# TensorE's side products cut into single matmuls and laid out anew in every step; ScalarE copies the value bank out ahead of that block's first exponential

## The reference

```python
xn = group_norm(x)                                   # 32 groups, no gain
xs = reshape(xn, (B, T, C))                          # B 16, T 1024, C 512
q, k, v = (einsum('btc,hcd->bhtd', xs, W) for W in (Wq, Wk, Wv))   # 8 heads of 64
att = softmax(einsum('bhtd,bhsd->bhts', q, k) / 8, axis=-1)
out = einsum('bhts,bhsd->bhtd', att, v)              # 1024 x 1024 scores per head
out = transpose(out, (0, 2, 1, 3)).reshape(B, T, -1) @ Wproj + bproj
return x + reshape(out, (B, C, H, W))
```

## Time and profile before

| | us |
|---|---|
| median of 3 runs (4952.30 to 4955.85) | 4953.66 |
| the profiled execution, first to last instruction | 4946.9 |
| PE busy | 4705.1 (95%) |
| ACT busy | 2886.6 (58%) |
| DVE busy | 2775.5 (56%) |
| POOL busy | 2326.6 (47%) |

### The profile page before, as it was taken

The page is one execution under the profiler, slowest core; times in us unless marked ns, Lnnn a source line. Parts: engine busy times, 40 slices in busy tenths (PEclk is TensorE's granted clock), DMA queues, the critical chain, the costliest instruction groups (busy, mean ns, idle before and its releaser), DMA issues.

```text
span 4946.9 us, 73065 instructions
## 1 busy us (share of the span) xinstructions
PE 4705.1 (95%) x20608; PEld 3505.4 (71%) x20608; DVE 2775.5 (56%) x5284; ACT 2886.6 (58%) x5507; POOL 2326.6 (47%) x1837
## 2 busy tenths in 40 slices
PE   7999999999999999999999999999999999999998
PEld 5777767777676776767767677676776767767675
DVE  5655646556465564655646556465564655646454
ACT  4665646556465564655646566464664646656465
POOL 2444545445454454544545445454444545445455
PEclk9999999999999999999999999999999999999999
DMA  2111111111111111111111111211112111111101
GB/s 69 34 37 55 31 53 35 46 46 32 52 34 50 43 34 54 31 53 41 32 54 35 51 41 30 63 28 53 37 30 62 35 49 35 32 61 34 53 23 51
DMA packets 156934, 212.71 MB, mean 43 GB/s; under 512 B 56544, under 2 KB 57568, under 8 KB 156512
## 3 DMA queue, kind: packets, MB, share of 16 engines
...
## 4 chain that ended last, share of the span: by engine, by line
issue 50%; POOL 42%; PE 6%; POOLq 1%; ACT 1%; DVE 0%; DMA 0%; SPq 0%; ACTq 0%; DVEq 0%
POOL prob_l L1031 32%; POOL o L1048 6%; POOL res L1054 3%; PE bank L517 1%; PE bank L561 1%; POOLq L1030 1%; POOL rstd L1023 1%; PE bank L578 1%; PE bank L690 1%; PE bank L692 1%; PE bank L691 1%; PE bank L571 0%; PE bank L572 0%; POOLq L1047 0%; DMA xs<-in_x 0%
## 5 line engine op out<-in xcount | busy, mean ns | idle before, releaser
L1031 POOL TENSOR_TENSOR prob_l<-prob,prob_h 128x512 fp32r<-128x512 f32 x1408 | 1803.5, 1288 | 2470.5 <-ACT prob_h L710 2452.6
L710 ACT ACTIVATE prob<-bank 128x512 f32<-128x512 f32 x2048 | 1237.6, 604 | 1698.6 <-PE bank L572 1579.3
L864 DVE TENSOR_REDUCE smax<-bank 128x1 f32<-128x512 f32 x2048 | 1349.1, 684 | 1012.6 <-PE bank L578 997.8
L710 ACT ACTIVATE prob_h<-bank 128x512 fp32r<-128x512 f32 x2048 | 1236.7, 604 | 198.6 <-PE bank L692 154.9
L690 PE MATMUL bank<-prob_h,vh 128*128 128x512 f32 x2048 | 832.6, 407 | 117.9 <-ACT acc L781 99.3
L578 PE MATMUL bank<-k_hl,q_hh 128*128 128x512 f32 x2048 | 802.5, 436 | 33.6 <-DVE smax L864 30.4
L571 PE MATMUL bank<-q_hh,k_hl 128*128 128x512 f32 x2048 | 824.0, 402 | 0.5 <-ACT prob_h L710 0.5
L572 PE MATMUL bank<-q_lm,k_h 65*128 65x512 f32 x2048 | 813.8, 397 | 0.0
L692 PE MATMUL bank<-prob_l,vh 128*128 128x512 f32 x2048 | 809.6, 395 | 0.0
L691 PE MATMUL bank<-prob_h,vl 128*128 128x512 f32 x2048 | 809.0, 395 | 0.0
L803 DVE TENSOR_TENSOR prob_l<-prob,prob_h 128x512 fp32r<-128x512 f32 x640 | 508.0, 804 | 511.9 <-ACT prob_h L710 511.8
...
## 6 DMA issues: line engine op xcount, KB each, us to landing
xs<-in_x SPq DMA_DIRECT2D x128, 256.0 KB, 2.8
q_hh<-q_hh SPq DMA_DIRECT2D x256, 128.0 KB, 2.2
k_hl<-k_h SPq DMA_DIRECT2D x256, 128.0 KB, 2.4
inv_b<-inv_dram SPq DMA_DIRECT2D x256, 128.0 KB, 2.8
res<-in_x SPq DMA_DIRECT2D x128, 256.0 KB, 2.7
out_x<-res SPq DMA_DIRECT2D x128, 256.0 KB, 2.0
q_lm<-q_lm SPq DMA_DIRECT2D x256, 2.0 KB
den<-acc SPq DMA_DIRECT2D x256, 2.0 KB, 1.7
```

Source lines behind the costliest of these rows:

```text
L710: return nc.scalar.activation(out, ps[ST + bank][:, :], ACT.Exp, scale=SCALE)
L864: nc.vector.tensor_reduce(smax[:, j:j + 1], ps[SM + j % 2][:, :], AX.X, ALU.max).then_inc(rows_used, 1)
L1031: nc.gpsimd.tensor_tensor(prob_l[:, r3, :], prob[:, ring2, :], prob_h[:, r3, :].bitcast(F32), ALU.subtract).then_inc(prob_l_pool, 1)
```

## The change

- `WORK` gives, for each slot, a tuple of pieces (kind, half, number of single matmuls, bank); row products are pieces too (`("row", n)`) and `MAXIMA` is gone. A projection can stop after any matmul and go on in the next slot. Banks no longer alternate by count, but are named.
- q and k for the next head are made in the step before it (`qk`), in slots 0 to 4. `qn` is left in head 4 (which makes head 5's `qk` and head 6's `qn`; the kind `double`) and in head 5 (head 7's; `ahead`). The prologue makes `qk` alone.
- Row products are ordered by halves of k (`row_of`), 16 a step as before. They stand at the end of slots 5 to 14 in most steps.
- The side work ahead of the value product stays in slots 0 and 8. ACT and DVE keep one order in all steps (`FIRST` is gone).
- ACT: `copy_out` in slots 7 and 15 stands ahead of both exponentials.
- `mt` is a transpose instead of a matmul with the identity.
- The group mean's aggregation in head 3 moves from slot 5 to 6, and one wait is added on POOL in head 0.

The lines of "values" shown are slots 7 to 14, those of "ahead" slots 7 and 8, those of "tokens" slots 14 and 15, that of "next" slot 0. "tokens" has two row products in each of slots 7 and 8 as well. The last two pieces are of ACT's `step` and of PE's `entry`.

```diff
-    "plain": ((1, "mt", 1, 0, 1), (10, "mt", 0, 0, 1), (10, "qn", 0, 0, 3), (12, "qn", 1, 0, 3),
-        (12, "qn", 0, 3, 4), (13, "qn", 1, 3, 4)),
...
-MAXIMA = {
-    "plain": (0, 0, 2, 1, 1, 1, 2, 0, 1, 2, 1, 2, 1, 1, 1, 0),
-    "values": (0, 0, 2, 1, 2, 0, 2, 0, 1, 1, 2, 2, 1, 0, 2, 0),
-    "tokens": (0, 1, 1, 1, 1, 1, 1, 1, 1, 2, 1, 2, 1, 2, 0, 0),
...
+    "double": (
+        (("qk", 0, 8, 0), ("mt", 1, 1, 1)),
+        (("qk", 0, 4, 0),),
+        (("qk", 1, 6, 1),),
+        (("qk", 1, 6, 1),),
+        (("qn", 0, 2, 0), ("row", 1)),
+        (("qn", 0, 2, 0), ("row", 1)),
+        (("qn", 0, 1, 0), ("row", 1)),
+        (("qn", 0, 1, 0), ("row", 2)),
+        (("qn", 0, 6, 0), ("row", 1)),
+        (("row", 2),),
+        (("qn", 1, 2, 1), ("row", 2)),
+        (("mt", 0, 1, 0), ("qn", 1, 2, 1), ("row", 1)),
+        (("qn", 1, 3, 1), ("row", 1)),
+        (("qn", 1, 5, 1), ("row", 2)),
+        (("row", 2),),
+        (),
+    ),
...
+    "values": (
...
+        (("v", 0, 6, 0), ("row", 1)),
+        (("v", 1, 8, 1), ("row", 1)),
+        (("v", 1, 6, 1), ("row", 2)),
+        (("v", 1, 6, 1), ("row", 1)),
+        (("v", 1, 4, 1), ("row", 2), ("mt", 0, 1, 0)),
+        (("row", 2),),
+        (("row", 2),),
+        (("row", 2),),
...
+    "ahead": (
...
+        (("row", 2),),
+        (("qn", 0, 3, 0), ("row", 2)),
...
+    "tokens": (
...
+        (("xt", 4, 4, 1),),
+        (),
+    ),
+    "next": (
+        (("mt", 1, 1, 0), ("xt", 5, 4, 1)),
...
+                    if i % TT == TT - 1:
+                        copy_out(s, i // TT)
                     if not (end and ahead):
                         r3 = ring3(s, i + AHEAD)
                         act.wait_ge(scores_ready, s.heads(BLOCKS, ahead, j + 1))
                         lo_wait(act, s, i + 1)
                         exp_to(prob[:, j % 2, :], r3)
-                    if i % TT == TT - 1:
-                        copy_out(s, i // TT)
...
-                    nc.tensor.matmul(w[0:4, 0:P], nmax[:, a * 4:(a + 1) * 4], ident[:, :],
-                                     start=True, stop=True).then_inc(mt_done, 1)
+                    nc.tensor.transpose(w[0:4, 0:P], nmax[:, a * 4:(a + 1) * 4], ident[:, :]).then_inc(mt_done, 1)
```

More of the change, by code:

```diff
@@ L356, in start_taken @@
         def start_taken(eng, kind, a):
-            n = plan.place["start", 0, (kind, a)]
-            eng.wait_ge(taken[n % 2], n // 2 + 1)
+            bank, before = plan.place["start", 0, (kind, a)]
+            eng.wait_ge(taken[bank], before + 1)
         def tile_count(s, t, credit=16):
@@ L513, in _ @@
         def _(pe):
-            def split_product(bank, cols, pairs, start, stop):
-                n = len(pairs)
-                for j, (w, m) in enumerate(pairs):
-                    last = nc.tensor.matmul(ps[bank][:, cols], w, m, start=start and j == 0,
-                                            stop=stop and j == n - 1)
-                return last
             def entry(kind, a, lo, hi, bank, before, head, wait):
@@ L771, in step @@
                         exp_to(prob_h[:, r3, :], r3).then_inc(prob_h_ready, 1)
-                    if not late:
-                        for kind, a in s.done(i):
-                            take_in_step(s, kind, a)
+                    for kind, a in s.done(i):
+                        take_in_step(s, kind, a)
             def copy_out(s, tc):
```

352 lines of the change are left out of this document (236 added, 116 removed), and 9 rows, old and new, of the table WORK.

## The result

| | before | after |
|---|---|---|
| median of 4 runs, us | 4954.76 | 5234.48 |
| span of the profiled execution, us | 4946.9 | 5229.7 |
| mean granted clock of TensorE | 0.994 | 0.972 |
| stretches at half clock in this span: number, us in all | 12, 58.0 | 79, 293.5 |

The changed kernel is 5.6% slower: ratio 1.0564, 95% interval 1.0549 to 1.0579. The forecast was 1.6% slower, 5035 us, and its range ended at 5095. The direction was right, the size was not: 283 us were added to the profiled span where I had 79.

A forecast was written before the change was run, and what follows sets the result against it. PE, busy 95% of the span, was taken as the bound, near its own pace. 4946.9 us + 54 (stops less savings) + 25 (clock) = 5026, with 6.8 for the median 5033, said as 5035; range 4905 to 5095.

The forecast's parts named there:

- Waits for `acc`, 143 us gone: The value product's waits for ACT's copy go, with the copy earlier and side work in front as cover: 143 us.
- `mt`, 40 us: The second pass of each of 256 `mt` goes, 0.15 us a piece: 40 us (bounds 0 and 79).
- Chains a to d: PE stops behind, in turn: taking projections (2.3 us), slot 7's `prob_l`, the maxima's row (0.5 to 1.4), taking values and tokens.
- chain b: Slot 7's `prob_l` holds DVE's queue 0.5 us longer through the earlier copy; slot 8's row products stop, 2.1 us in head 5.
- Head 5 and head 6 were then called "0": Step lengths of heads 5 and 6: new stops of 2.1 and 4.5 us offset by what goes, change 0.
- its 1.95 us on `acc`: Head 0, slot 0: PE's stop between scores and value product goes, 1.95 us of the step's -2.3.
- Heads 1 to 3: Step lengths: heads 1 and 2 +1.2 us each, head 3 +0.5, from new stops less old ones and `mt`'s 0.3.
- The clock, +25 us: Half the large new stops bring a half-clock stretch losing 1.5 to 1.9 us: +25 us (bounds -15 and +75).
- 46 stops of the right size: New stops about as long as 1.95 us: head 4 slot 10, head 7 slot 0, head 6 slots 7 and 8.
- much slower, 5105: Rival, chance 0.06: every stop over 1.5 us brings the slow clock, with late exponentials behind it, +70 us.
- Sum: Step changes of all heads together +54 us, with the clock's +25 on top.
- Signs named in advance: Trace signs: `acc` waits under 15 us, row products on `smax` over 200, head 4's step 37, head 0's 57, slot 13 DMA waits.

The follow-up runs named there:

- a_copyback: The changed kernel with the copy of the value bank again between the slot's two exponentials: 5201.8 us, ratio 1.0508.
- b_mt: The kernel before with one edit, `mt` as a transpose instead of a product with the identity: 4860.4 us, ratio 0.9816.
- a_fill: The changed kernel with 315 more matmuls that nobody reads, ahead of waiting row products in heads 5 and 6: 5185.4 us, ratio 1.0472.
- a_pool10: The changed kernel with block 10's `prob_l`, made in slot 7, on POOL instead of DVE: 5161.7 us, ratio 1.0430.
- a_fix: a_pool10 with four more repairs in the tables of heads 4, 5 and 7: 5075.7 us, ratio 1.0250.

## Why the prediction was right or wrong

- *Waits for `acc`, 143 us gone.* Right in the changed kernel (3.2 us left), though the 111.7 us and 121 times that I started from hold 12.4 us of weight loads. Its cause was wrongly shared out: I gave it to the copy with side work as cover; `a_copyback` shows that the layout does it alone.
- *`mt`, 40 us.* The mechanism was right and the size wrong: 91 us by `b_mt`, outside my upper bound of 79 too. The step that failed is the reading of the earlier trace rows: a price must be taken from the end of the pace before to the start of what follows, so with the late start of the first pass in it.
- *Chains a to d.* Where I followed a chain, the stop came at its place: head 4 slot 10 2.2 us (2.3), heads 1 and 2 slot 9 0.9 (0.9), head 5 slot 8 2.3 (2.1), head 7 slot 0 2.3 (2.3), head 3 slot 7 1.5 (1.5). Heads 1 and 2 had 0.8 and 0.7 us more, forecast as 0.7 on the row's DMA and 1.3 on maxima; all of it was on maxima, in slots 12 and 13. The DMA came last only in head 3 (0.7) and in 6 of 15 steps of head 4. Head 6's slot 2 had 1.4 instead of 0.6, and its slot 8 2.1 instead of 1.6. For chain b the stop was right and its price tag was not: I had the earlier copy hold DVE's queue 0.5 us longer everywhere. Against `a_copyback`, slot 7's `prob_l` ends no later in heads 3, 5 and 6, 0.5 us later in heads 4 and 7 and 1.3 in heads 1 and 2, mostly as POOL's `o` is under way when it starts or not.
- *Stops that I missed.* Head 5 slot 10 (2.1 us, the bank of `mt` 0), head 7 slot 14 (2.0, two row products that wait for maxima), head 0 slot 0 (0.9), and the loop's jump (2.9 us, 14 times). Together these are 8 us a batch, over 110 in all. I had looked for late DVE work only where row products were packed, not where a bank is asked for again one slot after an `mt`, and I didn't look at PE's own sequencer at all. Head 5 and head 6 were then called "0": +3.7 and +2.8 were measured. Head 0 lost its 1.95 us on `acc` as forecast and got the jump instead: +0.2 for -2.3.
- *Heads 1 to 3.* The forecast of +1.2 and +0.5 was met, in part by luck: the two `mt` gave 0.76 us a step where I had 0.3. Against it stand, in heads 1 and 2, 0.4 us of half clock that I had not put there (their stops were 3.3 us, 2.95 + 0.5 forecast), and in head 3 larger stops.
- *The clock, +25 us (bounds -15 and +75).* This term was off by the largest factor: half-clock stretches went from 58.0 to 293.5 us, and the loss in them from 17 to 122 us, +105, outside my upper bound. I counted 46 stops of the right size and took half; 39 of them brought a stretch (9 of 16 in head 4, all 30 in heads 6 and 7). Another 34 stretches stood behind stops that I had not counted: head 5's slots 8 and 10 (5 and 11 of 15), head 7's slot 14 (11) and the jump (7). My rival "much slower, 5105" had every large stop bring one, and was nearer. `a_fill` shows that this cost is real and separable.
- *Sum.* In the profiled spans: `mt` -97, stops +250, half clock +105, together +258 of +283. The forecast's +79 was made of `mt` -40, stops +94 and clock +25. So the step that failed is the sum of the new stops, 156 us too small, above all by the four places that it left out; the clock's term is second, 80 us too small, and `mt` took 57 us back. What the remaining 25 us are is not shown.
- *Signs named in advance.* `acc` under 15 us, row products on `smax` over 200 us, head 4's stop, head 7's slot 0, and the lower clock in heads 6 and 7 came as said; head 0 at 57 us did not (60.5), nor head 4 at 37 (38.1), nor a DMA in front of slot 13 in heads 1 and 2. The 200 us on `smax` hold in the view of the earlier trace rows, with the weight loads in it (597); the matmuls alone have 193.1.

Open is why single repairs give back a third of their gain or all of it, and in two runs more than that. Each trace names the next wait, but a rule that foretells it I don't have: of eight runs on the new layout, only `a_pool10` and `a_fix` fell into my ranges.
